# Windowed attention on one core: the values of all sixteen heads in one block, the projection two steps later

## The chip, the cores and the metric

The program runs on one core of one Trainium2 chip. The metric is the device time of the whole program in microseconds (us). Only the attention phase of the first layer, about an eighth of the program, is changed.

## The reference, cut to what matters

Two layers follow each other; each is `x + s * silu(f)` with an attention `s` and a feed-forward part `f`. The changed part is the attention of layer 0, on a normalised `x` of 2 batches of 2048 tokens, 512 wide, with 16 heads of 32:

```python
    x = L0_attn_x
    xn = _layernorm(x, axis=-1)
    s = _L0_attn_ref(xn, L0_attn_Wq, L0_attn_Wkv, L0_attn_Wk, L0_attn_Wv, L0_attn_Wo)
...
        mask = (ki <= qi) & ((qi - ki < WINDOW) | (ki < PERSIST))
        scores = jnp.einsum('bqhd,bkhd->bhqk', q, k) * scale
        scores = jnp.where(mask[None, None], scores, jnp.finfo(scores.dtype).min)
        attn = jax.nn.softmax(scores, axis=-1)
        out = jnp.einsum('bhqk,bkhd->bqhd', attn, v).reshape(B, S, D)
        return out @ Wo
```

WINDOW is 128 and PERSIST is 16: a query sees the 128 keys up to itself and the first 16 keys of its batch. All else (queries, keys and values themselves, a routed and a shared feed-forward part, the second layer) is done in other phases, which the change leaves as they are.

## The kernel before, in words

The phases run one after the other: `phase_front`, `phase_attend`, `phase_experts`, `phase_mix`, `phase_last`. `phase_attend` goes over 32 tiles of 128 queries (`TILES`), and in a tile over 16 heads (`NH`). One head of one tile is a step, `s = 16 u + h`. Every engine has its own hand-written program over the same steps (`STEPS`) and waits on counting semaphores, so the order of work on an engine is that of its code. `tile_of(s, offset)` says for which tile u a piece of work falls on step s, namely at `s = 16 u + offset`. An offset over 15 falls among the heads of the next tile. Below, "step 5" is head 5 of a tile, and the work that is left over from the tile before is named by the step on which it falls.

What a step does, engine by engine:

- **PE** (TensorE). `score(s + 3)` (L873): 128 queries against 288 keys, with 96 rows, into one of three banks `a_psS`. `turn(s)`: waits for the exponentials of step s, also on even steps; on odd steps it transposes the two heads just done into one of three banks `a_psP` (L890, four transposes). `values(u, g)` (L903): the product with the values for four heads, eight matmuls 32 columns wide that go to four column groups of the array, added up in the one bank `a_psO`. [...] `turn_sums` (L913): transposes of the probabilities of the 16 persistent keys and of the inverse row sums. `spread` (L931): a product with a 0/1 matrix `a_sel` that lays the 16 inverse sums over 512 columns, into the bank `a_psXY`. `pers_values` (L919): values of the persistent keys, added to `a_psO`. `project(u, c)` (L105 to L107 of the helper `mm3`): a quarter of the output projection into `a_psXY`.
- **DVE** (VectorE). `top(s + 3)` (L1033): masks and scales a bank of scores into one of three tiles `a_sm` and finds the row minimum. `copy_out` (L1044): copies a bank of transposes to `a_pT`, for the steps 1, 5, 9, 13, 15. `divide` (L1057): `a_psO` times the inverse sums, which gives `a_o`. `out_lo` (L1061): the low half of `a_o`. `finish` (L1068): copies the projection out.
- **ACT** (ScalarE). `exps(s + 2)` (L978): the exponentials of a head into `a_pr`. `copy_out` (L988) for the steps 3, 7, 11. `sums_out` (L994): the result of `turn_sums` to `a_xT`, which `spread` waits for. `inverse_out` (L1000): copies what `spread` made to `a_rb`. `out_hi` (L1006): the high half of `a_o`, which `out_lo` waits for.
- **POOL** (GpSimd) has other work in the same phase: when heads 0 to 7 of a tile have their exponentials it gathers 16 columns of each (L805) and issues three indirect DMAs (L810); after heads 8 to 15 it does so again, and then stores a finished tile (L827). For four tiles it also copies keys of the second batch (L711).

Before, the four groups of `values` fall on steps 8, 12, 0 and 4 (one group each; the last two among the heads of the next tile), `turn_sums` on step 1, `spread` on step 3, `pers_values` on step 4, `divide` on step 5, `out_hi` and `out_lo` on step 6, and the four parts of the projection on steps 9 to 12. The ring `a_pT` holds 8 tiles of transposes (`TR`).

Of the kernel before, what the change touches and what calls it, by code (L numbers as in the profile page):

```python
# [20 lines left out]
P = 128  # L21
# [11 lines left out]
NH, HD = 16, 32  # L33
# [574 lines left out]
def phase_attend(nc, env):  # L608
# [6 lines left out]
    ctx, sb, ps, sem = scope(nc)  # L615
    R = 4
    QR = 3
    N = TILES * NH
    HH = NH // 2
    GH = 4  # L620
    NGR = NH // GH
# [3 lines left out]
    LAG = 5  # L625
    SR = 3
    PR = 3
    TR = 8
    CH = (0, P + PERSIST)
    ON_ACT = (1, 3, 5)  # L630
    ON_DVE = tuple(p for p in range(HH) if p not in ON_ACT)
    with ctx:
# [3 lines left out]
        kp = sb("a_kp", [ST, B, NH, PERSIST], F32R)  # L636
        vd = sb("a_vd", [P, B, 2, HD])
        vp = [sb(f"a_vp{i}", [P, 2, HH, HD]) for i in range(B)]
        sel = sb("a_sel", [NH, NGR, GH, HD])
        mask = [sb(f"a_mask{i}", [P, W]) for i in range(4)]  # L640
        rl = [sb(f"a_rl{i}", [P, P]) for i in range(2)]
        wo = [sb(f"a_wo{h}", [P, KC, D], F32R) for h in range(2)]
# [110 lines left out]
        xT = [sb(f"a_xT{i}", [P, 3 * P]) for i in range(2)]  # L753
# [16 lines left out]
        X_AT = 17  # L770
# [17 lines left out]
        def bank(u, p):  # L788
            return psP[order[u, p] % PR]

        STEPS = range(N + 32 - NH)

        def tile_of(s, offset):

            u, rest = divmod(s - offset, NH)
            return u if rest == 0 and 0 <= u < TILES else None
# [60 lines left out]
        @block.tensor  # L857
        def _(pe):
            pe.wait_ge(cleared, 6)

            def score(s):
                u, h = divmod(s, NH)
                if h == 0:
                    pe.wait_ge(q_in[u % QR], 48 * (u // QR + 1))
                    pe.wait_ge(kv_in[u % R], 64 * (u // R + 1))
                    if u == 0:
                        pe.wait_ge(pers_ready, PERS)
                    if BT <= u < BT + R:
                        pe.wait_ge(pers_ready, PERS + u - BT + 1)
                if s >= SR:  # L870
                    pe.wait_ge(s_used, s - SR + 1)
                lo, hi = slots(u)
                pe.matmul(psS[s % SR][:, :].rearrange("p (a k) -> p a k", a=2), qs[u % QR][:, h, :],  # L873
                          ks[:, lo:hi + 1:hi - lo, h, :], start=True, stop=True).then_inc(s_full, 1)

            def bank_free(u, p):
                i = order[u, p]
                if i >= PR:
                    copied_out(pe, *turns[i - PR])

            def turn(s):
                u, h = divmod(s, NH)
                p = h // 2
                pe.wait_ge(p_ready, s + 1)
                if h % 2 == 0:
                    return
                bank_free(u, p)
                for hh in (h - 1, h):
                    for c in range(2):
                        ins = pe.transpose(bank(u, p)[:, (2 * (hh % 2) + c) * P:(2 * (hh % 2) + c + 1) * P],  # L890
                                           pr[hh // HH][:, hh % HH, CH[c]:CH[c] + P], env.ident[:, :])
                ins.then_inc(pT_full, 1)

            def values(u, g):
                for p in (2 * g, 2 * g + 1):
                    copied_out(pe, u, p)
                if g == 0 and u:

                    pe.wait_ge(o_ready, u)
                for c, i in enumerate(slots(u)):  # L900
                    for j in range(GH):
                        h = GH * g + j
                        ins = pe.matmul(psO[j * HD:(j + 1) * HD, g, :], vb[i][:, h, :],  # L903
                                        pT[(u * HH + h // 2) % TR][:, (2 * (h % 2) + c) * P:(2 * (h % 2) + c + 1) * P],
                                        start=(g == 0 and c == 0), stop=False, skip_group_check=True)
                ins.then_inc(pv_done, 1)

            def turn_sums(u):
                pe.wait_ge(pp_ready, 2 * u + 2)
                pe.wait_ge(rl_ready, u + 1)  # L910
                bank_free(u, HH)
                for i, src in enumerate((pp[0], pp[1], rl[u % 2])):
                    ins = pe.transpose(bank(u, HH)[:, i * P:(i + 1) * P], src[:, :], env.ident[:, :])  # L913
                ins.then_inc(x_full, 1)

            def pers_values(u):
                for half in range(2):
                    for g in range(2):
                        ins = pe.matmul(psO[:, 2 * half + g, :],  # L919
                                        vp[u // BT][:, half, GH * g:GH * (g + 1), :].rearrange("p h d -> p (h d)"),  # L920
                                        xT[u % 2][:, half * P:(half + 1) * P], start=False,
                                        stop=(half == 1 and g == 1), skip_group_check=True)
                ins.then_inc(pers_done, 1)

            def spread(u):
                pe.wait_ge(x_out, u + 1)
                if u:

                    pe.wait_ge(y_ready, u)
                for g in range(NGR):  # L930
                    ins = pe.matmul(psR[:, g, :], sel[:, g, :, :].rearrange("p j d -> p (j d)"),  # L931
                                    xT[u % 2][0:NH, 2 * P:3 * P], start=True, stop=True)
                ins.then_inc(spread_full, 1)

            def project(u, c):
                if c == 0:
                    pe.wait_ge(o_split, u + 1)
                    if u == 0:
                        pe.wait_ge(wo_split, 1)
                ins = mm3(pe, psXY[:, :], [oT[h][:, c, :] for h in range(2)], [wo[h][:, c, :] for h in range(2)],  # L940
                          c == 0, c == KC - 1)
                if c == KC - 1:
                    ins.then_inc(y_full, 1)

            for s in range(SR):
                score(s)
            for s in STEPS:
                if s + SR < N:
                    score(s + SR)
                if s < N:  # L950
                    turn(s)
                for g in range(NGR):
                    if (u := tile_of(s, GH * g + GH - 1 + LAG)) is not None:
                        values(u, g)
                if (u := tile_of(s, X_AT)) is not None:
                    turn_sums(u)
                if (u := tile_of(s, X_AT + 2)) is not None:
                    spread(u)
                if (u := tile_of(s, X_AT + 3)) is not None:
                    pers_values(u)  # L960
                for c in range(KC):
                    if (u := tile_of(s, X_AT + 8 + c)) is not None:
                        project(u, c)

        @block.scalar
        def _(act):
# [14 lines left out]
            def copy_out(s):  # L981
                u, h = divmod(s, NH)
                p = h // 2
                if h % 2 and p in ON_ACT:
                    if u:
                        act.wait_ge(pv_done, (u - 1) * NGR + p // 2 + 1)
                    act.wait_ge(pT_full, u * HH + p + 1)
                    act.activation(pT[(u * HH + p) % TR][:, :], bank(u, p)[:, :], ACT.Copy).then_inc(pT_act, 1)  # L988

# [20 lines left out]
            for s in STEPS:  # L1010
                if s + SR - 1 < N:
                    exps(s + SR - 1)
                if s < N:
                    copy_out(s)
                if (u := tile_of(s, X_AT)) is not None:
                    sums_out(u)
                if (u := tile_of(s, X_AT + 3)) is not None:
                    inverse_out(u)
                if (u := tile_of(s, X_AT + 5)) is not None:
                    out_hi(u)  # L1020

        @block.vector
        def _(dve):
# [13 lines left out]
            def copy_out(s):  # L1037
                u, h = divmod(s, NH)
                p = h // 2
                if h % 2 and p in ON_DVE:  # L1040
                    if u:
                        dve.wait_ge(pv_done, (u - 1) * NGR + p // 2 + 1)
                    dve.wait_ge(pT_full, u * HH + p + 1)
                    dve.tensor_copy(pT[(u * HH + p) % TR][:, :], bank(u, p)[:, :]).then_inc(pT_dve, 1)  # L1044

# [28 lines left out]
            for s in STEPS:  # L1074
                if s + SR < N:
                    top(s + SR)
                if (u := tile_of(s, X_AT - 3)) is not None:
                    invert(u)
                if s < N:
                    copy_out(s)  # L1080
                if (u := tile_of(s, X_AT + 4)) is not None:
                    divide(u)
                if (u := tile_of(s, X_AT + 5)) is not None:
                    out_lo(u)
                if (u := tile_of(s, X_AT + 12)) is not None:
                    finish(u)


# [1581 lines left out]
```

## Time and profile before

| | us |
|---|---|
| median of 3 runs | 4498.79 (4495.98 to 4507.62) |
| the profiled execution, its own time | 4549.09 |
| its span | 4547.1 |
| attention: first to last `score` | 389.3 to 942.4 |
| PE, DVE, ACT, POOL busy in 389 to 942 | 486, 365, 382, 234 |
| granted TensorE clock in 389 to 942 | 0.97 of full speed |

A row of a timeline is one instruction, or a few of the same kind in a row (xN): its start, its duration, and in brackets the idle time of its engine before it with what ended that. The busy time of PE is counted from modelled ends: a transpose is recorded with 0.27 us, though the next one starts 0.11 us later. So what a piece of work costs PE is read from start to start. LDWEIGHTS, the loading of weights, has rows of its own (PEld), which overlap the matmuls.

### The profile page before, as it was taken

Reading aid. Unit: us, or ns where it says so; the run is one execution under the profiler, and the core shown is the slowest. Engines: PE = TensorE matmul, PEld = TensorE weight load, DVE = VectorE, ACT = ScalarE, POOL = GpSimd, SP = SyncE. Lnnn points to the kernel's source line nnn. Section 1 sums busy time; section 2 is a strip of 40 time slices with the busy share of each in tenths; the row PEclk is TensorE's granted clock in tenths of the full one; section 3 lists DMA queues with packets and bytes.
Section 4 is the critical chain, followed back from the end, with each engine's and each line's share of the span. In section 5 each row is a group of like instructions: output and inputs, shape, how many; then the busy total and the mean of one; then the engine's idle time right before and its main releaser. Section 6 shows DMA issues by size and latency. Waiting matters only on the chain. (4 is left out here: it accounts for less than half of the span.)

```text
span 4547.1 us, 69223 instructions
## 1 busy us (share of the span) xinstructions
PE 4214.5 (93%) x23045; PEld 3571.8 (79%) x23046; DVE 2097.8 (46%) x4010; ACT 1663.2 (37%) x3234; POOL 1354.6 (30%) x2020
## 2 busy tenths in 40 slices
PE   6975888879999999999997999998799999999998
PEld 5864666669989999998985777776578888788887
DVE  4457666644444444444444544453343333343333
ACT  2214666644334444444432333331232222222222
POOL 0012444445555555555551233333100000000000
PEclk8877999989999999999998999998899999999999
DMA  5767676636555556555554533431423222321221
GB/s 188 282 237 173 118 141 122 126 88 131 114 122 124 128 121 135 123 125 128 120 118 140 181 123 130 140 134 58 146 75 104 98 87 71 102 95 63 98 82 48
DMA packets 351911, 561.40 MB, mean 123 GB/s; under 512 B 33089, under 2 KB 198625, under 8 KB 347490
## 3 DMA queue, kind: packets, MB, share of 16 engines
q1 hardware_dynamic: 282770, 394.19, 29.3%
q0 software_dynamic: 68944, 164.62, 16.8%
q8 instruction: 120, 1.97, 0.2%
q14 instruction: 77, 0.63, 0.1%
HBM read 384.36 MB, written 174.34 MB: 123 GB/s over the span
## 5 line engine op out<-in xcount | busy, mean ns | idle before, releaser
L1227 POOL DMA_INDIRECT acc_d<-e_yw,e_to x208 | 336.0, 1615 | 284.9 <-ACT e_yw L1384 268.4
L2289 POOL DMA_DIRECT2D out<-d_res x32 | 17.4, 543 | 1304.8 <-DVE d_res L2521 1304.8
L2468 DVE TENSOR_TENSOR d_h<-d_sg,d_psU 128x512 f32<-128x512 f32 x144 | 98.9, 687 | 520.3 <-PE d_psU L107 461.9
L978 ACT ACTIVATE a_pr<-a_sm,a_nmax 128x272 f32<-128x272 f32 x512 | 264.0, 516 | 167.1 <-DVE a_nmax L1033 137.6
L105 PE MATMUL e_psG<-e_gu,e_xT 128*128 128x352 f32 x832 | 289.6, 348 | 11.4 <-DVE e_xT L1438 9.3
L1446 DVE TENSOR_TENSOR e_h<-e_sg,e_psU 128x352 f32<-128x352 f32 x208 | 108.3, 521 | 394.3 <-ACT e_sg L1397 379.9
L1033 DVE CUSTOM_DVE_ANT_0 a_sm<-a_psS,a_mask 128x272 f32<-128x272 f32 x512 | 212.7, 432 | 156.6 <-PE a_psS L873 140.2
L107 PE MATMUL e_psG<-e_gu,e_xT 128*128 128x352 f32 x832 | 271.9, 327 | 0.0
L106 PE MATMUL e_psG<-e_gu,e_xT 128*128 128x352 f32 x832 | 271.4, 326 | 0.0
L105 PE MATMUL e_psU<-e_gu,e_xT 128*128 128x352 f32 x832 | 271.0, 326 | 0.0
L106 PE MATMUL e_psU<-e_gu,e_xT 128*128 128x352 f32 x832 | 269.6, 324 | 0.0
L105 PE MATMUL e_psY<-e_wd,e_hT 128*128 128x512 f32 (+1 forms) x624 | 265.7, 426 | 1.2 <-DVE e_hT L1429 1.2
L107 PE MATMUL e_psU<-e_gu,e_xT 128*128 128x352 f32 x832 | 266.3, 320 | 0.0
L1197 POOL DMA_INDIRECT e_xs<-xn_d,e_idx x209 | 210.2, 1006 | 174.3 <-POOL e_idx L1194 168.3
L2396 ACT ACTIVATE d_hT<-d_h 128x512 fp32r<-128x512 f32 x144 | 91.0, 632 | 458.9 <-DVE d_h L2468 400.9
L107 PE MATMUL e_psY<-e_wd,e_hT 128*128 128x512 f32 (+1 forms) x624 | 247.1, 396 | 0.0
L1397 ACT ACTIVATE e_sg<-e_psG 128x352 f32<-128x352 f32 x208 | 96.4, 463 | 409.3 <-PE e_psU L107 406.5
L106 PE MATMUL e_psY<-e_wd,e_hT 128*128 128x512 f32 (+1 forms) x624 | 245.4, 393 | 0.0
L2390 ACT ACTIVATE d_sg<-d_psG 128x512 f32<-128x512 f32 x144 | 86.0, 598 | 423.0 <-PE d_psG L107 423.0
L1378 ACT ACTIVATE e_hT<-e_psH 128x384 fp32r<-128x384 f32 x208 | 102.1, 491 | 371.3 <-PE e_psY L107 199.5
L105 PE MATMUL d_psG<-d_x,d_gu 128*128 128x512 f32 x576 | 225.2, 391 | 12.6 <-DMA d_x<-xT_d 12.5
L105 PE MATMUL d_psU<-d_x,d_gu 128*128 128x512 f32 x576 | 227.5, 395 | 0.0
(429 smaller groups left out, 12067.1 us busy)
## 6 DMA issues: line engine op xcount, KB each, us to landing
d_gu_raw<-in_wgu SPq DMA_DIRECT2D x144, 512.0 KB, 3.2
qk_d<-f_qk SPq DMA_DIRECT2D x32, 1024.0 KB
a_q<-qk_d SPq DMA_DIRECT2D x96, 256.0 KB
a_k<-qk_d SPq DMA_DIRECT2D x96, 256.0 KB
e_rawgu<-in_w_gate SPq DMA_DIRECT2D x32, 704.0 KB
e_rawgu<-in_w_up SPq DMA_DIRECT2D x32, 704.0 KB
b_gu_raw<-in_wgu SPq DMA_DIRECT2D x40, 512.0 KB, 3.9
xT_d<-f_xT SPq DMA_DIRECT2D x16, 1024.0 KB
```

The costliest lines, as they stand in the source:

```text
L105: pe.matmul(out, lhs[0], rhs[1], start=first, stop=False, **kw)
L106: pe.matmul(out, lhs[1], rhs[0], start=False, stop=False, **kw)
L107: return pe.matmul(out, lhs[0], rhs[0], start=False, stop=last, **kw)
L978: act.activation(pr[half][:, h % HH, :], sm[s % SR][:, :], ACT.Exp, bias=nmax[s % SR][:, :], scale=-1.0, accum_out=rs[u % 2][:, h:h + 1]). ...
L1033: dve.tensor_tensor_reduce(out=sm[s % SR][:, :], in0=psS[s % SR][:, PERSIST:2 * KW], in1=m[:, :], scale=-SCALE, scalar=3.0e38, op0=ALU.add ...
L1197: pool.indirect_dma_start(rows[:, :], None, env.xn_d, bass.IndirectOffsetOnAxis(ap=idx[k][:, :].bitcast(U32), axis=0))\
L1227: pool.indirect_dma_start(env.acc_d, bass.IndirectOffsetOnAxis(ap=to[:, :].bitcast(U32), axis=0), yw[:, :], None, compute_op=ALU.add).then ...
L1378: act.activation(hT[0][:, :, :], psH[:, :, :], ACT.Copy).then_inc(hT_hi, 1)
L1397: act.activation(sg[:, :], psG[:, 0:M], ACT.Silu).then_inc(sg_ready, 1)
L1446: dve.tensor_tensor(hv[:, :], sg[:, :], psU[:, 0:M], ALU.mult).then_inc(h_ready, 1)
L2396: act.activation(h2[q % 2][0][:, :], hv[q % 2][:, :], ACT.Copy).then_inc(h_hi, 1)
L2468: ins = dve.tensor_tensor(hv[q % 2][:, :], sg[q % 2][:, :], psU[:, :], ALU.mult)
```

## The change

All values of a tile are now one block: the four groups follow each other on step 4 (offset `NH - 1 + LAG` = 20), where the last group stood. What comes after is moved: `spread` from step 3 to 5, `pers_values` from 4 to 6, `inverse_out` from 4 to 6, `divide` from 5 to 7, `out_hi` and `out_lo` from 6 to 8, the projection from steps 9 to 12 to steps 12 to 15, and `finish` from step 13 to step 0 of the tile after. The ring `a_pT` grows from 8 to 10 tiles, since the transposes of steps 1 and 3 of the next tile are copied before the block has read the old ones; `slot_free` is the wait that belongs to it. The matrix `a_sel` now has 128 rows of which rows 16 to 127 are zero, so that `spread` is a product over 128 rows instead of 16. `STEPS` is one longer.

```diff
-    TR = 8
+    TR = 10
...
-        sel = sb("a_sel", [NH, NGR, GH, HD])
+        sel = sb("a_sel", [P, NGR, GH, HD])
...
+        def slot_free(eng, u, p):
+
+            i = u * HH + p - TR
+            if i >= 0:
+                eng.wait_ge(pv_done, i // HH * NGR + i % HH // 2 + 1)
+
+        STEPS = range(N + 33 - NH)
...
-                                    xT[u % 2][0:NH, 2 * P:3 * P], start=True, stop=True)
+                                    xT[u % 2][:, 2 * P:3 * P], start=True, stop=True)
...
-                for g in range(NGR):
-                    if (u := tile_of(s, GH * g + GH - 1 + LAG)) is not None:
+
+                if (u := tile_of(s, NH - 1 + LAG)) is not None:
+                    for g in range(NGR):
                         values(u, g)
                 if (u := tile_of(s, X_AT)) is not None:
                     turn_sums(u)
-                if (u := tile_of(s, X_AT + 2)) is not None:
+                if (u := tile_of(s, X_AT + 4)) is not None:
                     spread(u)
-                if (u := tile_of(s, X_AT + 3)) is not None:
+                if (u := tile_of(s, X_AT + 5)) is not None:
                     pers_values(u)
                 for c in range(KC):
-                    if (u := tile_of(s, X_AT + 8 + c)) is not None:
+                    if (u := tile_of(s, X_AT + 11 + c)) is not None:
                         project(u, c)
...
-                    if u:
-                        act.wait_ge(pv_done, (u - 1) * NGR + p // 2 + 1)
+                    slot_free(act, u, p)
...
-                if (u := tile_of(s, X_AT + 3)) is not None:
+                if (u := tile_of(s, X_AT + 5)) is not None:
                     inverse_out(u)
-                if (u := tile_of(s, X_AT + 5)) is not None:
+                if (u := tile_of(s, X_AT + 7)) is not None:
                     out_hi(u)
...
-                    if u:
-                        dve.wait_ge(pv_done, (u - 1) * NGR + p // 2 + 1)
+                    slot_free(dve, u, p)
...
-                if (u := tile_of(s, X_AT + 4)) is not None:
+                if (u := tile_of(s, X_AT + 6)) is not None:
                     divide(u)
-                if (u := tile_of(s, X_AT + 5)) is not None:
+                if (u := tile_of(s, X_AT + 7)) is not None:
                     out_lo(u)
-                if (u := tile_of(s, X_AT + 12)) is not None:
+                if (u := tile_of(s, X_AT + 15)) is not None:
                     finish(u)
```

On PE, from the transposes of the sums (step 1) on, a tile before the change reads as follows (a row is one kind of matmul with its count, out<-in by the program's names):

```order
L913 MATMUL a_psP<-ident,a_rl 128x128
L873 MATMUL a_psS<-a_k,a_q 128x288 x2
L890 MATMUL a_psP<-ident,a_pr 128x128 x4
L931 MATMUL a_psXY<-a_xT,a_sel 128x128 x4
L873 MATMUL a_psS<-a_k,a_q 128x288
L903 MATMUL a_psO<-a_pT,a_v 32x128 x8
L919 MATMUL a_psO<-a_xT,a_vp 128x128 x4
L873 MATMUL a_psS<-a_k,a_q 128x288
L890 MATMUL a_psP<-ident,a_pr 128x128 x4
L873 MATMUL a_psS<-a_k,a_q 128x288 x2
L890 MATMUL a_psP<-ident,a_pr 128x128 x4
L873 MATMUL a_psS<-a_k,a_q 128x288
```

After it (line numbers are six higher, so L909 is `values`, L937 `spread` and L925 `pers_values`):

```order
L919 MATMUL a_psP<-ident,a_rl 128x128
L879 MATMUL a_psS<-a_k,a_q 128x288 x2
L896 MATMUL a_psP<-ident,a_pr 128x128 x4
L879 MATMUL a_psS<-a_k,a_q 128x288
L909 MATMUL a_psO<-a_pT,a_v 32x128 x32
L879 MATMUL a_psS<-a_k,a_q 128x288
L896 MATMUL a_psP<-ident,a_pr 128x128 x4
L937 MATMUL a_psXY<-a_xT,a_sel 128x128 x4
L879 MATMUL a_psS<-a_k,a_q 128x288
L925 MATMUL a_psO<-a_xT,a_vp 128x128 x4
L879 MATMUL a_psS<-a_k,a_q 128x288
L896 MATMUL a_psP<-ident,a_pr 128x128 x4
```

`spread` has moved behind the block and has a whole block, a score and four transposes more between it and the transposes of the sums; the block is followed by a score, `spread`, another score and `pers_values`.

On DVE, around `divide` and `out_lo`, before the change:

```order
L1044 COPY a_pT<-a_psP 128x512
L1057 TENSOR_TENSOR a_o<-a_psO,a_rb 128x512
L1033 ISA a_sm,a_nmax<-a_psS,a_mask 128x272
L1033 ISA a_nmax 128x1
L1061 TENSOR_TENSOR a_oT<-a_o,a_oT 128x512
L1033 ISA a_sm,a_nmax<-a_psS,a_mask 128x272
```

After it:

```order
L1049 COPY a_pT<-a_psP 128x512
L1039 ISA a_sm,a_nmax<-a_psS,a_mask 128x272
L1039 ISA a_nmax 128x1
L1039 ISA a_sm,a_nmax<-a_psS,a_mask 128x272
L1039 ISA a_nmax 128x1
L1062 TENSOR_TENSOR a_o<-a_psO,a_rb 128x512
L1039 ISA a_sm,a_nmax<-a_psS,a_mask 128x272
L1039 ISA a_nmax 128x1
L1066 TENSOR_TENSOR a_oT<-a_o,a_oT 128x512
L1039 ISA a_sm,a_nmax<-a_psS,a_mask 128x272
L1039 ISA a_nmax 128x1
L1049 COPY a_pT<-a_psP 128x512
```

`divide` no longer stands right behind the copy of step 5; `out_lo` still stands one `top` behind `divide`, and the next `top` and the copy of step 9 stand behind `out_lo`.

## Rows read from the trace of the kernel before

**Rows 1.** One line: every score matmul (durations in ns min/median/max, first and last start).

```profile
L873 PE MATMUL a_psS<-a_k,a_q x512: 289/378/610, 389.3 to 942.4; 96*128 96x288 f32 x171
```

**Rows 2.** Waits from 400 to 942 us: waiter, releaser, total us, times, longest.

```profile
DVE a_sm L1033 <- PE a_psS L873: 139.0, 142, 2.8
...
PE a_psXY L931 <- ACT a_xT L994: 19.4, 30, 1.4
...
PE a_psO L903 <- DVE a_o L1057: 18.3, 27, 0.7
```

**Rows 3.** Timeline of PE in one tile: start, duration, [idle before <-releaser].

```profile
645.41 0.64 PE L903 MATMUL a_psO<-a_pT,a_v 128*32 128x128 f32 x16
645.98 0.50 PE L105 MATMUL a_psXY<-a_wo,a_oT 128*128 128x512 f32 x1
...
646.78 0.29 PE L873 MATMUL a_psS<-a_k,a_q 96*128 96x288 f32 x1
646.91 0.60 PE L890 MATMUL a_psP<-ident,a_pr 128*128 128x128 f32 x4
...
648.46 0.64 PE L903 MATMUL a_psO<-a_pT,a_v 128*32 128x128 f32 x16
649.32 0.40 PE L873 MATMUL a_psS<-a_k,a_q 96*128 96x288 f32 x1 [0.22 <-DVE a_nmax L1033]
649.97 0.66 PE L890 MATMUL a_psP<-ident,a_pr 128*128 128x128 f32 x4 [0.25 <-ACT a_pr L978]
...
650.46 0.38 PE L913 MATMUL a_psP<-ident,a_pp 128*128 128x128 f32 x2
...
652.71 1.15 PE L931 MATMUL a_psXY<-a_xT,a_sel 16*128 16x128 f32 x8 [0.65 <-ACT a_xT L994]
653.79 0.40 PE L873 MATMUL a_psS<-a_k,a_q 96*128 96x288 f32 x1
654.12 0.65 PE L903 MATMUL a_psO<-a_pT,a_v 128*32 128x128 f32 x16
654.69 1.16 PE L919 MATMUL a_psO<-a_xT,a_vp 128*128 128x128 f32 x8
655.61 0.38 PE L873 MATMUL a_psS<-a_k,a_q 96*128 96x288 f32 x1
655.83 0.60 PE L890 MATMUL a_psP<-ident,a_pr 128*128 128x128 f32 x4
656.18 0.52 PE L873 MATMUL a_psS<-a_k,a_q 96*128 96x288 f32 x2
```

**Rows 4.** Timeline of POOL in the same tile.

```profile
647.75 0.98 POOL L810 DMA_INDIRECT ids_d<-a_pair,a_slot  x1 [0.16 <-issue]
...
651.26 0.58 POOL L827 DMA_DIRECT2D s_d<-a_y  x1
...
656.26 0.29 POOL L805 COPY a_pp<-a_pr 128x128 f32<-128x128 f32 x1 [4.01 <-ACT a_pr L978]
```

**Rows 5.** Timeline of ACT in the same tile.

```profile
649.30 0.52 ACT L978 ACTIVATE a_pr<-a_sm,a_nmax 128x272 f32<-128x272 f32 x1 [0.90 <-DVE a_nmax L1033]
...
652.16 0.49 ACT L994 ACTIVATE a_xT<-a_psP 128x384 f32<-128x384 f32 x1 [0.82 <-PE a_psP L913]
...
653.61 0.52 ACT L978 ACTIVATE a_pr<-a_sm,a_nmax 128x272 f32<-128x272 f32 x1 [0.35 <-DVE a_nmax L1033]
```

**Rows 6.** Timeline of DVE in the same tile.

```profile
652.16 0.44 DVE L1033 CUSTOM_DVE_ANT_0 a_sm<-a_psS,a_mask 128x272 f32<-128x272 f32 x1 [1.47 <-PE a_psS L873]
...
653.13 0.43 DVE L1033 CUSTOM_DVE_ANT_0 a_sm<-a_psS,a_mask 128x272 f32<-128x272 f32 x1
...
656.13 0.44 DVE L1033 CUSTOM_DVE_ANT_0 a_sm<-a_psS,a_mask 128x272 f32<-128x272 f32 x1 [1.35 <-PE a_psS L873]
656.53 0.69 DVE L1044 COPY a_pT<-a_psP 128x512 f32<-128x512 f32 x1
657.14 0.68 DVE L1057 TENSOR_TENSOR a_o<-a_psO,a_rb 128x512 f32<-128x512 f32 x1
```

More of the change, by code:

```diff
@@ L789, in bank @@
             return psP[order[u, p] % PR]
-        STEPS = range(N + 32 - NH)
+        def slot_free(eng, u, p):
[3 more added lines that the diff above has]
+        STEPS = range(N + 33 - NH)
         def tile_of(s, offset):
```

## The prediction

> **What bounds the kernel now.** Only the attention phase is touched, so I read the row of all scores first: 511 intervals between the first and the last of 512 take 553.1 us, so a tile of 16 heads takes 17.3 us [rows 1]. In the small table of times no engine fills that: PE's busy time, 88% of the phase, counts modelled ends, and DVE and ACT are busy for two thirds of it. The phase is a ring of waits: a score goes to DVE, ACT, and back to PE for its transposes, with three banks at each place.
>
> The table of waits shows where the ring stops. DVE waits 139 us in all for scores, 4.3 us per tile; PE waits 19.4 us for ACT in front of `spread` and 18.3 us for `divide` in front of the first group of values [rows 2].
>
> The timelines of one tile show what lies behind the first two of these. The group of values at 648.46 is followed by a score at 649.32 and by the transposed sums at 650.46 [rows 3]. The results of both are taken up at the same moment, 652.16, by DVE after 1.47 us and by ACT after 0.82 us of idle time [rows 5, 6]. Both had been issued long before: PE did the work, but its completion came up to 2.8 us late. The group at 654.12 behaves otherwise: the score at 655.61 is with DVE after 0.52 us [rows 3, 6]. The difference that I see is POOL: its indirect DMAs and its store run from 647.75 to 651.84, and it is idle for the 4.01 us before 656.26 [rows 4]. In the timelines of the tiles I looked at, the groups on steps 8 and 0, which fall into POOL's two bursts of indirect DMAs, have late results behind them, and the groups on steps 12 and 4, which fall between the bursts, have none.
>
> **The change, part by part.** I follow one tile of the new order, with t = 0 at the score of step 5, which comes right behind the block. Intervals, all from start to start:
>
> - PE: a score costs 0.13 us when it streams (646.78 to 646.91) and 0.22 behind another kind (655.61 to 655.83); four transposes 0.36 (655.83 to 656.18), or 0.49 after a wait (649.97 to 650.46); a part of the projection 0.80 behind values (645.98 to 646.78), and my estimate for behind a score or transposes is 0.70 to 0.78; `pers_values` 0.92 (654.69 to 655.61) [rows 3].
> - ACT: exponentials 0.52 and a copy 0.48, and from the start of the exponentials to the transposes that wait for them 0.67 (649.30 to 649.97) [rows 3, 5].
> - DVE: a `top` 0.4, a copy or `divide` 0.61 (656.53 to 657.14); from a `top` to its exponentials 0.48 (653.13 to 653.61); from a score to its `top` 0.52, and from transposes to their copy 0.70 (655.83 to 656.53) [rows 3, 5, 6].
>
> *Values.* A group costs 0.57 us from its start to the next matmul [rows 3]; the sixteen records go in four fours, which with (0.64 - 0.27) / 3 between them makes 0.44 to 0.48 and leaves about 0.13 for the exit. Entering costs 0.1: a score and the way into the values take 0.33 (653.79 to 654.12), a score and the way into transposes 0.22. One block costs 4 x 0.44 + 0.24 = 2.0 us where four groups cost 4 x 0.67 = 2.7. The upper bound is 2.2, with 0.48.
>
> *Spread.* It costs 1.08 us now (652.71 to 653.79) against 0.92 for `pers_values`, which has the same eight records over 128 rows [rows 3]. With 128 rows I take 0.91. Its bounds are 0.9 and, if the rows cost nothing and the exit stays, 1.08.
>
> *First stretch.* PE streams: score 0.22, transposes 0.38, `spread` 0.91, score 0.13, `pers_values` 0.92, score 0.13, so the transposes of step 7 start at 2.69. ACT copies them from 3.39 to 3.87, does the exponentials of step 10 until 4.39 and `out_hi` until 4.9. `divide` ran from 3.37 to 4.05, in time. `out_lo` starts at 5.03, and the `top` behind it at 5.64. This is the wait that is late next. It gives exponentials at 6.12, and one copy and one `top` later, at 7.09, those of step 13, whose transposes start at 7.76.
>
> *Second stretch.* Now PE has a queue: transposes 0.49, projection 0.75, score 0.13, projection 0.70, score 0.13, transposes 0.36, projection 0.78: 11.10. The moved projection costs PE nothing more than before; it only fills other steps.
>
> *Third stretch.* The score at 11.10 gives a `top` at 11.55, `finish` from 11.9, the next `top` at 12.50 and exponentials, behind `sums_out`, at 13.04. The block waits for them until 13.75, takes 2.0 us, and the round closes at 15.75 us. The other wait that is gone, `spread` on `a_xT`, has the whole block as its cover; the values no longer wait for `divide`, which lies 13 steps ahead of the next block.
>
> The late results are the part that the sum costs at nothing. In this round the exponentials of step 15 start at 8.6, so POOL's second burst, which takes 4.1 us before (647.75 to 651.84) [rows 4], runs from about 9.7 to 13.9, and the block from 13.8 to 15.6. The first burst starts after the exponentials of step 7, near t = 1.3. The block stands in the gap between the bursts. If this cover fails, the price is that of the rivals below.
>
> *Ring of transposes and loads.* The copies of steps 5 and 7 wait for the block's first group. PE issues those transposes only behind the block, so nothing waits. Loads of keys hang on the last group, which stays on step 4. POOL's store waits for `finish`, near 12.6 here, when its burst is still running. Both cost nothing.
>
> I round 15.75 to 16.0, since I took each reaction time at its short end and the block near its lower bound. The gain per tile is 1.3 us. Over 31 tiles it is 40 us. The last tile has all its values in the tail, where three groups used to be done earlier: 1.3 us, with one step more some 2 us. Sum: -38 us.
>
> The profiled execution took 4549.1 us (span 4547.1), 50 us over the median of the runs shown. I make the sum there, 4549.1 - 38 = 4511, and carry the difference to the median: 4498.8 - 38 = **4461 us**.
>
> **The rivals.**
>
> *Late results come with POOL's bursts, values or not.* Then they stay, only behind other work. For this speaks that in the rows the lateness lies in a burst; against it, that scores issued in a burst just ahead of the values show no late `top` that I could find. In the round above, `pers_values` would be reported late (`divide` at about 4.1 instead of 3.4, hence the exponentials of step 11 about 0.4 us later), and in the second burst the score before 11.10 and those behind it would be handed over 1 us late. Together 1.5 us: 17.25 us per tile, no change, 4499 us.
>
> *Late results come with every block that a score follows.* This is the rival on the other side. The two groups with late results are also those that a score follows; the groups on steps 12 and 4 have a projection and `pers_values` behind them. The new block is always followed by a score. Price: with the 2.8 us seen behind the group at 648.46, the first `top` of the round is at 3.3 instead of 0.5; ACT then does the exponentials of steps 8 and 9, the inverse, the copy and step 10 in one row, `out_hi` ends at 6.8 instead of 4.9, and a tile takes 15.75 + 1.9 = 17.65 us. That is 0.35 us more than now, 11 us over the phase, 13 with the tail: 4512 us. It decides against the change when results are later than about 2.5 us; with 1.5 us most of the gain would stay. SBUF — State Buffer of the Trainium skill (section "SBUF: two separate sides") says that on the engine side only the port pair shared by DVE and GpSimd contends, and that PE and ACT never wait on anyone. By that rule POOL could not be what delays PE's results, and this rival would hold. The rows of this case, with lateness only inside POOL's bursts, speak against the rule but do not exclude it.
>
> *PE becomes the bound.* If `out_lo` and `finish` are overtaken better than I think, PE's own stream is left: 16 scores 2.3, 8 sets of transposes 3.2, sums 0.3, block 2.0, `spread` and `pers_values` 1.8, projection 3.0, which is 12.6, plus the waits for exponentials in front of the block and of step 11, 2.3: 14.9 us per tile, 2.4 less, 4425 us.
>
> **How the numbers follow.** Forecast 0.60 (15.5 to 16.5 us per tile, 4445 to 4477); bursts without values 0.17; every block 0.13; PE's stream 0.10. Faster by over 0.3% means below 4485, and 0.3% is about what a measurement of this kernel can tell from no change: all of the forecast's own range and PE's stream, and some of the bursts' case where the lateness is smaller, 0.73. Within 0.3%: 0.14. Slower: 0.13. The range for 8 in 10 reaches from 4430 to 4505: it leaves out half of the fastest case and most of the slowest.
>
> **What would show it.** In the profile of the changed kernel the 512 scores should span about 515 us. The wait of DVE for scores should fall from 139 us to under 100, ACT's wait in front of `sums_out` and PE's in front of `spread` and of the values on `divide` should be gone. A `top` should follow the score behind the block by about 0.5 us. `spread` to the next score should be 0.91. New or larger: PE's wait for exponentials in front of the block and on step 11, and a `top` held behind `out_lo`. The prediction is wrong in its main step if scores behind the block are taken up 2 us late (second rival), or if `top` waits over 1 us inside POOL's bursts although no values ran (first rival).

## The result, and the profile after

The changed kernel takes 4519.35 us (median of 20 runs) where the kernel before takes 4505.99 (20 runs): ratio 1.0029, 95% interval 1.0022 to 1.0036, so 13 us slower. The forecast was 4461 and faster. The profiled execution of the changed kernel has an own time of 4522.8 us, 3 us over its median. That of before stood 43 us over this median of before, and that difference turned out to matter. It is none of these 20 runs, and the record does not say on which chip it was taken.

The row of all scores answers to [rows 1]; they now span 535.3 us, 16.76 per tile, and 17.06 in the steady part:

```profile
L879 PE MATMUL a_psS<-a_k,a_q x512: 288/379/607, 386.5 to 921.8; 96*128 96x288 f32 x171
```

The waits from 400 to 942 us answer to [rows 2]:

```profile
ACT a_pr L985 <- DVE a_nmax L1039: 135.3, 214, 1.7
DVE a_sm L1039 <- PE a_psS L879: 73.7, 155, 1.9
DVE a_sm L1039 <- ACT a_pr L985: 59.9, 58, 1.5
PEld a_psP L896 <- ACT a_pr L985: 44.3, 95, 0.8
```

The waits of `spread` for `a_xT` and of the values for `divide` are gone, as forecast. What the forecast does not have shows in the windows of one tile (columns: busy us and instructions of PE, PEld, DVE, ACT, POOL, then granted clock, DMA share, GB/s):

```profile
645.20:647.20 2.00, 1.58 (x14) 1.39 (x12) 1.41 (x5) 1.68 (x6) 1.57 (x2) 1.00 1.23 185
647.20:649.20 2.00, 1.25 (x6) 0.66 (x6) 1.63 (x5) 1.39 (x5) 0.34 (x1) 1.00 1.12 235
649.20:651.20 2.00, 1.88 (x9) 1.59 (x10) 1.55 (x9) 1.66 (x7) 0.00 (x0) 0.76 1.28 183
651.20:653.20 2.00, 2.00 (x7) 1.61 (x7) 0.82 (x2) 1.02 (x5) 1.26 (x2) 0.50 1.22 200
653.20:655.20 2.00, 2.00 (x12) 1.71 (x11) 1.39 (x6) 1.05 (x4) 1.39 (x3) 0.89 1.01 308
```

On steps 8 to 11 PE has only scores and a few transposes (1.25 us busy of 2.00). Behind that the granted clock falls to half, 1.2 of 2.4 GHz, for 3.4 us, just where the projection now stands. The timeline of PE shows the price: products of 512 columns start 0.43 us apart (651.62 to 652.05) instead of 0.24 (654.65 to 654.89).

```profile
650.28 1.12 PE L896 MATMUL a_psP<-ident,a_pr 128*128 128x128 f32 x4
651.05 0.78 PE L105 MATMUL a_psXY<-a_wo,a_oT 128*128 128x512 f32 x1
651.62 0.63 PE L106 MATMUL a_psXY<-a_wo,a_oT 128*128 128x512 f32 x1
652.05 0.63 PE L107 MATMUL a_psXY<-a_wo,a_oT 128*128 128x512 f32 x1
...
654.33 0.48 PE L105 MATMUL a_psXY<-a_wo,a_oT 128*128 128x512 f32 x1
654.65 0.41 PE L106 MATMUL a_psXY<-a_wo,a_oT 128*128 128x512 f32 x1
654.89 0.40 PE L107 MATMUL a_psXY<-a_wo,a_oT 128*128 128x512 f32 x1
```

This returns in every steady tile, 29 times behind the first tile; the granted clock of the phase is 0.90. In the profile of before it was 0.97, and in that of e1 below, where nothing is late, 0.99. The block (32 products, recorded as 64) costs 1.88 us, and the score behind it reaches DVE in 0.55 us; no result is late:

```profile
657.69 1.95 PE L909 MATMUL a_psO<-a_pT,a_v 128*32 128x128 f32 x64 [0.17 <-ACT a_pr L985]
659.57 0.40 PE L879 MATMUL a_psS<-a_k,a_q 96*128 96x288 f32 x1
```

### The profile page after: what moved, and what is told of

It is laid out like the page before. It is cut to its first block and busy times, and to the rows that moved or that the text cites. A ratio compares the mean times of both kernels' runs of the same rounds, so it can differ in the third digit from the quotient of the medians.

```text
span 4520.9 us, 69284 instructions
## 1 busy us (share of the span) xinstructions
PE 4205.3 (93%) x23045; PEld 3592.9 (79%) x23046; DVE 2102.9 (47%) x4010; ACT 1663.8 (37%) x3234; POOL 1349.6 (30%) x2020
## 5 line engine op out<-in xcount | busy, mean ns | idle before, releaser
L2294 POOL DMA_DIRECT2D out<-d_res x32 | 17.3, 541 | 1304.8 <-DVE d_res L2526 1304.8
```

## The experiments

The runs came to five chips, and the kernel before is not equally fast on them: 4503 and 4507 us on two, 4547, 4539 and 4539 on three. I call these the first and the second kind. Ratios are always to before on the same chip. Each of the five chips was used in one session only, so a difference between chips and one between sessions cannot be told apart; "kind of chip" stands for both. Theories: **A**, late results made the profiled execution of before a bad base; **C**, the clock eats the gain; **D**, the block starves DVE and ACT.

### Before once more, and single parts of the change (first kind)

> The kernel before, unchanged, profiled once more. Theory A (the profiled execution of before was not like its timed ones: completions of values late by 1.3 to 3.2 us behind two groups per tile, which cost time only there): the timed runs are at 1.000 of before, and this profile too has an own time some 40 us over the timed median, with late results behind the groups on steps 8 and 0. Rival B (that one execution was a stray): this profile is near 4506 us, scores span about 515 us instead of 553, and a top follows the score behind such a group by 0.5 us.

Unchanged kernel: 4505.1 us, ratio 1.0001 (0.9990 to 1.0013); the span of its profile is 4500.6 us.

```profile
L873 PE MATMUL a_psS<-a_k,a_q x512: 289/377/608, 386.4 to 907.2; 96*128 96x288 f32 x171
```

```profile
650.10 0.66 PE L890 MATMUL a_psP<-ident,a_pr 128*128 128x128 f32 x4 [0.17 <-ACT a_pr L978]
650.69 1.15 PE L931 MATMUL a_psXY<-a_xT,a_sel 16*128 16x128 f32 x8
651.77 0.40 PE L873 MATMUL a_psS<-a_k,a_q 96*128 96x288 f32 x1
...
655.95 0.65 PE L903 MATMUL a_psO<-a_pT,a_v 128*32 128x128 f32 x16 [0.70 <-DVE a_o L1057]
```

The scores span 520.8 us instead of the 553.1 of [rows 1]; a steady tile takes 16.46 us instead of 17.3. `spread` follows its transposes without the 0.65 us of [rows 3]; the wait for `divide` is still there. Rival B of this run holds for this chip: nothing is late here. Late results are best counted by the time from the start of the last transpose of the sums to the start of `sums_out`: it is 0.57 us at most here, and over 1 us in 30 of 32 tiles of the profile of before. The wait of DVE for scores, 140.7 us from 400 to 880, is not smaller than that of before in the same window (125.0), so I had read too much into that row of [rows 2].

> Before, with one part of the change alone: the 0/1 matrix has 128 rows, so spread is a product over 128 rows instead of 16. If leaving the narrow shape costs what the rows say (1.08 against 0.92 us), PE gets 0.16 us per tile back, 5 us in all if PE is on the path at that place, 0 if the wait for the transposed sums in front of it hides it: 4501 to 4506 us, ratio 0.999 to 1.000. Slower only if a product over 128 rows costs more than one over 16.

```diff
-        sel = sb("a_sel", [NH, NGR, GH, HD])
+        sel = sb("a_sel", [P, NGR, GH, HD])
-                                    xT[u % 2][0:NH, 2 * P:3 * P], start=True, stop=True)
+                                    xT[u % 2][:, 2 * P:3 * P], start=True, stop=True)
```

4490.6 us, ratio 0.9966 (0.9954 to 0.9979); tiles take 16.07 us. More than expected, 0.40 us per tile where one exit at 0.16 was priced.

```profile
645.08 0.66 PE L890 MATMUL a_psP<-ident,a_pr 128*128 128x128 f32 x4 [0.18 <-ACT a_pr L978]
645.57 1.06 PE L931 MATMUL a_psXY<-a_xT,a_sel 128*128 128x128 f32 x8
646.38 0.38 PE L873 MATMUL a_psS<-a_k,a_q 96*128 96x288 f32 x1
```

From these transposes to the score behind `spread` it is 1.30 us, and in the rows of e1 1.67 (650.10 to 651.77): `spread` itself takes 0.81 instead of 1.08, and starts 0.10 sooner. Repeated as e15 on another chip of the first kind it gave 0.9962 (0.9947 to 0.9977):

> Before with the 128 rows alone, once more. Where before takes 4505: 4491, ratio 0.9966, as measured. Where before takes 4540: the late results of before should stay, since no values are moved, and the gain is 0 to 15 us: ratio 0.996 to 1.000.

> The changed kernel with the transposes of steps 7, 9 and 11 done twice into the same bank: 12 transposes more per tile, 1.1 us of PE work that gives nothing. Theory C (clock: the changed kernel leaves PE nearly idle on steps 8 to 11, the granted clock falls to half for 3.4 us in every tile behind that, 0.90 on average in the phase against 0.97 before, and this costs about 1.3 us per tile): with PE busier there the clock stays up more often, the mean in the phase rises towards 0.97, and the kernel is faster than the changed one, 4480 to 4510 us, although it does more. Theory D (starvation: the block of 2.0 us keeps scores from DVE and ACT and the three banks are empty behind it): more PE work in that place can only cost, 4520 to 4550 us.

```diff
-                for hh in (h - 1, h):
+                for _ in range(2 if p in (3, 4, 5) else 1):
+                    for hh in (h - 1, h):
```

4487.7 us, ratio 0.9954 (0.9941 to 0.9967), against 1.0029 for the change: twelve transposes more per tile, and 32 us less. Tiles take 16.00 us, and the clock in the phase is 0.99, with no half-clock stretch behind the first tile. D cannot give this.

> The changed kernel with the four parts of the projection on steps 10 to 13 instead of 12 to 15; all else as in the change. Theory C (clock): PE has work in the quiet stretch, the half-clock stretch is rarer, and the kernel is faster than the changed one by 10 to 40 us, 4480 to 4510. Theory D (starvation behind the block): the projection is added where the ring is still refilling, so nothing is gained, 4515 to 4530.

```diff
-                    if (u := tile_of(s, X_AT + 11 + c)) is not None:
+                    if (u := tile_of(s, X_AT + 9 + c)) is not None:
```

4516.2 us, ratio 1.0025 (1.0016 to 1.0035): no cure, and outside the range of theory C. The time lies in the range of D, though it is not made by D: 19 half-clock stretches are left of 29, and a tile at full clock takes 16.0 us, 0.4 more than that of e16 below. The profile also holds the cleanest measurement. The clock falls in some tiles and not in others, and these windows are one tile each:

```profile
621.50:637.50 16.00, 13.70 (x145) 11.92 (x144) 11.15 (x42) 12.20 (x38) 7.35 (x12) 1.00 0.60 117
637.50:655.00 17.50, 15.20 (x145) 13.13 (x144) 11.85 (x43) 12.75 (x40) 7.76 (x13) 0.90 0.91 183
655.00:672.50 17.50, 15.19 (x145) 13.16 (x144) 11.50 (x41) 11.93 (x39) 7.77 (x13) 0.90 0.73 159
672.50:690.00 17.50, 15.20 (x144) 13.15 (x143) 11.39 (x41) 12.19 (x38) 7.76 (x13) 0.90 0.77 162
690.00:706.00 16.00, 13.69 (x145) 11.92 (x144) 11.51 (x43) 12.21 (x38) 7.75 (x13) 1.00 0.61 117
```

The same work takes 16.0 us at full clock and 17.5 with one half-clock stretch: 1.5 us per tile.

> The change without its 128 rows: spread is again a product over 16. On before the 128 rows gave 0.40 us per tile (16.46 to 16.06), so if the same wait is on the path here, tiles would be 0.2 to 0.4 us longer with the clock as in the change: 17.3, 4525 to 4535. If the period is tied to the half-clock stretch, the tile may stay near 17.0, or the clock may stay up when PE's work falls otherwise: 4490 to 4520.

With spread over 16 rows again: 4511.6 us, ratio 1.0018 (1.0006 to 1.0029) on a chip of the first kind. Tiles take 15.95 us at full clock and 17.7 with a half-clock stretch. The first of the two expectations, 4525 to 4535, was wrong; the time lies in the second range. At full clock the 128 rows are worth 0.4 us here too (15.56 in e16, with four transposes on top), but the order with them has 29 half-clock stretches, and this one 20.

### Less filling, other blocks, and a control (second kind, e16 on the first)

> The changed kernel with the transposes of step 9 alone done twice (4 more per tile, 0.36 us of idle work; the filled kernel above had 12). Theory C (clock): if this little is enough to keep the clock, tiles take about 15.7 us, less than the 16.0 of the filled one, and the time is near 4478; if it is not enough, tiles fall back to 17.1 with a stretch of half clock each, 4520. A share of tiles of either kind gives a value between. What excludes theory C is a time that is the changed kernel's plus the added work, with the clock up.

Only the transposes of step 9 are doubled (`p == 4`): 4497.2 us, ratio 0.9882 (0.9866 to 0.9898). Before took 4547 on this chip, which is how the two kinds came to light. Two repeats, e12 on the second kind and e16 on the first, were made with these expectations:

> The changed kernel with four transposes more per tile, once more. On a chip where before takes 4505: tiles of 15.55 us with the clock up, 4475 to 4482, ratio 0.994 to 0.995, and 35 to 45 us under the changed kernel on the same chip, which shows the price of the clock on one chip. On a chip like the last: 4497 again, 0.988, and if the clock is the matter the changed kernel beside it is 20 us slower.

> The changed kernel with four transposes more per tile, a third time. Where before takes 4505: 4475 to 4485, ratio 0.994 to 0.996, tiles of 15.55 us. Where before takes 4540: 0.988 again. If it is not under before on the first kind of chip, it does not beat both kernels everywhere.

e12: 4485.3 us, 0.9879 (0.9861 to 0.9897). e16: 4469.3 us, 0.9920 (0.9905 to 0.9935), with tiles of 15.56 us and these scores:

```profile
L880 PE MATMUL a_psS<-a_k,a_q x512: 292/378/606, 388.3 to 880.4; 96*128 96x288 f32 x171
```

The clock is 0.99 in the phase. Both repeats took less than was expected. This version is faster than both kernels on either kind of chip.

On the second kind it is not free of late results: the time from the last transpose of the sums to `sums_out` is over 1.1 us in 8 of 32 tiles of e12 and in 5 of e5, and in none of e16. e5 also has four half-clock stretches, so it missed the 4478 us expected of it. One of them in e12, with no values ahead of it but an indirect DMA on POOL:

```profile
671.73 0.27 PE L921 MATMUL a_psP<-ident,a_rl 128*128 128x128 f32 x1
671.99 0.96 POOL L817 DMA_INDIRECT ids_d<-a_pair,a_slot  x1 [0.30 <-issue]
672.97 0.49 ACT L1002 ACTIVATE a_xT<-a_psP 128x384 f32<-128x384 f32 x1 [0.62 <-PE a_psP L921]
```

> The control: the kernel before, whose clock is up nearly everywhere in the phase, with the same 12 extra transposes per tile on steps 7, 9 and 11. Theory C (clock): here they give nothing back and cost up to 1.1 us per tile, 35 us; since PE waits on some of these steps, 10 to 35 us: 4515 to 4540. If extra transposes helped for another reason than the clock (the order of waits, say), this would be at or under 4504 too.

The control, twelve transposes more in the kernel before: 4562.4 us, ratio 1.0037 (1.0024 to 1.0051), 15 us more than before on this chip, as theory C has it. The control is not a clean one: on this kind of chip before has half-clock stretches too, eight in its profile, and with the extra transposes there were still ten. Its results are late as in the profile of before, in 30 of 32 tiles. So the transposes do not help by themselves, but they do not prevent every fall of the clock either.

> The values in one block on step 4, with the 128 rows and the ring of 10, but spread, the persistent values, divide, the output halves, the projection and finish on their steps of before. If the block itself is the gain and the later projection the loss, this is faster than 4490 (before with 128 rows): the wait of the values for divide (22 us) goes and six narrow entries and exits per tile go, so 15.3 to 15.9 us per tile and 4460 to 4485, with the granted clock at 0.95 or more in the phase. If the block itself makes PE's quiet stretch (steps 5 to 8 then hold only scores and transposes), there are half-clock stretches here too and the time is 4500 to 4520.

The block with every later step at its place of before: 4524.1 us, 0.9956 (0.9943 to 0.9969), and 0.9962 in a repeat (e11). Tiles take 16.6 us at full clock, 18.2 with one half-clock stretch and 20.1 with two, eight stretches in all. The 15.3 to 15.9 that I expected of the block alone is not there, and not because of late results, of which the steady tiles of this profile have none:

```profile
712.80 1.96 PE L909 MATMUL a_psO<-a_pT,a_v 128*32 128x128 f32 x64
714.69 1.16 PE L925 MATMUL a_psO<-a_xT,a_vp 128*128 128x128 f32 x8
715.60 0.38 PE L879 MATMUL a_psS<-a_k,a_q 96*128 96x288 f32 x1
716.13 0.44 DVE L1039 CUSTOM_DVE_ANT_0 a_sm<-a_psS,a_mask 128x272 f32<-128x272 f32 x1 [2.66 <-PE a_psS L879]
```

Block and `pers_values` follow each other on step 4, so PE gives no score for 3.1 us and DVE waits 2.66. This is theory D, in this order and not in that of the change, where a score stands between them. At full clock the changed order, with its two further steps, is thus the faster one, 15.6 us (the third tile of its own profile, and e16) against 16.6. Both chips were of the second kind; the first was not tried.

> Before with 128 rows, and the values in two blocks of two groups, on steps 12 and 4; all else on its step of before, ring of 8. The wait of the first group for divide goes (22 us in all), and half of the narrow entries and exits, 0.25 us each pair: up to 0.7 + 0.5 us per tile under 16.07, so 15.2 to 15.8, 4463 to 4482. Work stays spread, so theory C expects no half-clock stretches beyond the few of before. If the gains of both waits are given back by exponentials coming late, 4490.

Two groups on step 12 and two on step 4: 4523.4 us, 0.9948 (0.9936 to 0.9961), in repeats 0.9959 (e10) and 0.9965 (e18). All three runs came to the second kind, and tiles take 16.95 us instead of the 15.2 to 15.8 expected. The clock is 0.99 in the phase, as theory C has it, and `sums_out` is never late, so neither the clock nor late results make these tiles long. Its timelines show another wait:

```profile
653.10 0.29 PE L873 MATMUL a_psS<-a_k,a_q 96*128 96x288 f32 x1
653.55 0.44 DVE L1033 CUSTOM_DVE_ANT_0 a_sm<-a_psS,a_mask 128x272 f32<-128x272 f32 x1 [1.59 <-PE a_psS L873]
653.94 0.69 DVE L1044 COPY a_pT<-a_psP 128x512 f32<-128x512 f32 x1
654.55 0.68 DVE L1068 COPY a_y<-a_psXY 128x512 f32<-128x512 f32 x1
655.15 0.43 DVE L1033 CUSTOM_DVE_ANT_0 a_sm<-a_psS,a_mask 128x272 f32<-128x272 f32 x1
655.73 0.37 PE L873 MATMUL a_psS<-a_k,a_q 96*128 96x288 f32 x1 [1.06 <-issue]
```

The two groups and a part of the projection stand between the score at 651.06 and that at 653.10, and DVE waits 1.59 us for the latter. It then has a copy and `finish` to do before the `top` at 655.15, and the score at 655.73 needs the bank which this `top` reads. The profile names no releaser for this wait; that it is the bank is my reading of the code. The same wait of 1.06 us in e6 is put down to DVE. From 400 to 880 us the waits of PE in front of scores for which no releaser is named come to 46.6 us, 1.6 per tile. So 16.95 us may well be the time of a tile on the first kind too, which no run tried.

### What makes results late, and the change on the second kind

> The changed kernel, unchanged. What before does depends on the chip: 4503 to 4506 us without late results, 4547 with them. Theory E (the late results are a matter of the chip and of the order of before; the changed order avoids them everywhere; the half clock is a matter of the changed order on any chip): the changed kernel takes 4515 to 4522 on any chip, so its ratio is 1.003 where before takes 4505 and 0.994 where before takes 4547, and its profile has one half-clock stretch of 3.4 us per tile. Rival: the changed kernel is also some 40 us slower on the other kind of chip, 4560, ratio 1.003 again.

The changed kernel on a chip of the second kind: 4521.2 us against 4538.8, ratio 0.9960 (0.9947 to 0.9974), with the same tiles of 17.0 us and a clock of 0.90. So the change takes the same time in both places; it is before that varies, and the sign of the result with it. e12 ran on the same chip: 36 us less, with four transposes more and the clock up.

> The kernel before with POOL's indirect DMAs behind the attention's last tile, once more. Where before takes 4540: if POOL's bursts make results late, tiles take 16.4 us and no top waits over 1 us for a score; if the lateness belongs to the values alone, tiles stay at 17.2. Where before takes 4505: 16.4 as in the run before, and nothing is told.

```diff
                 gather(u, 0)
-                scatter(u, range(3))
                 gather(u, 1)
-                scatter(u, range(3, TOPK))
...
+            for u in range(TILES):
+                scatter(u, range(TOPK))
```

(The copies and waits of the scatter move along.) The first run of it, e13, came to the first kind and took 4766.7 us with tiles of 16.46; e17 came to the second and took 4767.0, again with tiles of 16.46:

```profile
L873 PE MATMUL a_psS<-a_k,a_q x512: 289/377/606, 386.7 to 907.5; 96*128 96x288 f32 x171
```

The whole programs are slower because the DMAs now stand in a row behind the phase, as was expected. In the phase the kinds of chip no longer differ: the scores span 520.9 us in e13 and 520.8 in e17, and `sums_out` is late in neither. So POOL's bursts (the indirect DMAs and the three small copies that feed them, which were not tried apart) make the results late, on the second kind only. That no `top` would wait over 1 us was a bad sign to choose: they still do, up to 1.5 us, but as in e1, for scores that are issued late. Why these chips do it is open, and so is why the changed order has no late `sums_out` in e9, where its bursts fall on scores and transposes as well, and some in e5 and e12, four transposes later.

## Why the prediction was wrong

**What bounds the kernel.** Half right. The late results were real in the execution that I read, and POOL's bursts were the right suspect. SBUF — State Buffer of the Trainium skill (section "SBUF: two separate sides") says that PE and ACT never wait on anyone, and I had concluded that by this rule POOL could not be what delays PE's results. e17 shows that the conclusion does not follow. Whether the sentence of the page itself holds no run here shows: in these rows PE's products start in time, and what comes late is what the other engines see of their results. But the late results are worth 0.85 us per tile (17.3 against 16.46) and eight half-clock stretches, 32 us of the phase in all, and on the chips of the first kind they do not exist.

**The step that failed first: the base.** "I make the sum there, 4549.1 - 38 = 4511, and carry the difference to the median." The profiled execution stood 50 us over the median of the runs beside it. That was the sign that it had a cost which those had not, and 32 us of it is just the cost that I credited the change with removing (553.1 against 520.8 us for the scores in e1). Where it exists, the change is faster (4521 against 4539), by 18 us instead of 38.

**The step that failed in the sum: the clock.** Every PE duration was taken at full clock and the granted clock was no term, although I wrote that the projection "only fills other steps". At full clock the round was well sized: 15.75 us worked out, 16.0 forecast, 15.56 measured in e16 with four transposes on top, and 15.57 in the third tile of the changed kernel's own profile, before the clock first falls. Missing are 1.5 us per tile (e4), because the changed order leaves steps 8 to 11 thin on PE and the clock falls behind them; four transposes put there keep it up (e9 and e12, 4521 and 4485 us on one chip). From 16.46: 0.9 gained, 1.5 lost, 0.6 worse per steady tile. Less at the start of the phase, the scores span 14.5 us more (520.8 to 535.3), and 13.4 were timed.

**Values.** One block of 2.0 us, measured 1.88. Right. **Spread.** 0.91 forecast, 0.82 measured in the profile after (643.16 to 643.98). Mis-sized: on the path the 128 rows gave 0.40 us instead of 0.16 (e2), since `pers_values` was the wrong product to compare with and the way into the narrow shape was priced at nothing.

**Waits.** The two of [rows 2] on PE were gone. That of DVE for scores fell under 100 us as forecast (73.7), but this sign says nothing on late results: it is 140.7 in e1, which has none. The forecast new waits came: PE for exponentials on step 11 (0.62 us) and in front of the block (0.17), `out_lo` in front of a `top`.

**Rivals.** The second, on the slower side, gave 4512 and the measured sign, but by a mechanism that did not act: no result behind the block was late. The first, lateness inside bursts without values, is seen in e12 and e5, in some tiles, and not in the changed kernel. What keeps scores from DVE behind a block was none of the rivals; e6, where `pers_values` follows at once, takes about 1 us per tile more at full clock than the changed order. The clock was no rival, and should have been: [rows 1] to [rows 6] hold no granted clock, and the small table had 0.97 for the phase.

## What to carry to other kernels

Moving work out of a stretch of PE can cost more than the waits it removes, if what stays is so thin that the granted clock falls and the dense work stands right behind it: look at PE's busy share in windows of the new order, not only at its waits, and try a little idle work there (four transposes gave back 36 us on one chip). A profiled execution that stands 1% over the timed median has a cost of its own; find it before pricing an edit by it, and take a second profile on another chip. What follows a long block directly makes the block longer for the engines that wait for other work of PE (e6, e7).

## What was not expected of the hardware

The same program takes 4503 and 4507 us on two chips and 4539 to 4547 on three, each in a session of its own; the difference disappears (4766.7 and 4767.0 us on one of each) when 192 indirect DMAs of POOL leave the attention phase. One stretch of half clock per tile lasted 3.4 us and cost 1.5 us. The tiles of the change then take 17.04 to 17.09 us nearly all, where those of e14 take 15.9 to 17.7. `spread` over 16 rows costs PE 0.37 us more, way in and out included, than over 128 rows of which 112 are zero (e1, e2).
